# Second layer's row maxima: one of each two key blocks as a difference, its positive part on ScalarE, sum and maximum in one VectorE instruction

## The chip, the cores and the metric

The kernel runs on one core of one Trainium2 chip, in one launch. The metric is device time in microseconds (us): the median of several runs. A profiled execution gives the span from the first to the last instruction, and times below that are given as places ("at 1178.66 us") are us from the start of that span.

## The reference

Two transformer layers on 2048 tokens of 128 channels, all in fp32. The first is causal softmax attention with 16 heads of 8 channels and a linear layer; the second, where the change lies, is linear attention and then an attention whose heads mix experts. Cut to what matters here (8 heads, 5 experts, head size 64):

```python
q5 = (x @ Wq).reshape(b, t, H, E, DH)                 # k5 and v5 likewise from Wkv
q = jnp.einsum('bthed,bthe->bhtd', q5, sd_g)          # experts summed under gates
k = jnp.einsum('bthed,bthe->bhtd', k5, ss_g)
v = jnp.einsum('bthed,bthe->bhtd', v5, ss_g)
attn = jax.nn.softmax(jnp.einsum('bhid,bhjd->bhij', q * scale, k), axis=-1)
out = jnp.einsum('bhij,bhjd->bihd', attn, v)          # then Wo under a mask, summed over experts
```

The softmax is over 2048 keys of each query, without a causal mask, and subtracts each query's maximum before the exponential.

## The kernel before

Each engine runs its own list of instructions in order, and semaphores tie them. The order is set by one list of steps, `SEQ1` for the second layer: every engine walks through it and issues its part of each step. The list is merged from a regular foreground and from preparation steps that carry places in time (`preparation1`, `merge`). Those places come from numbers written by hand (`PROJ1`, `STAGE1`, `MAX1`).

The unit of the foreground is one S step: for a chunk of 512 queries, two tiles of 128 keys. TensorE makes two 128x512 blocks of scores, each from a main product (L775) and a correction product that also adds minus the row maximum (L776). ScalarE takes the exponential of both in one instruction of 1024 columns (L960). Two units later the V step multiplies with the values (L786), and in the D step VectorE adds 704 of the 1024 columns to the running denominator (L1283) and GpSimd the other 320 (L1383). A chunk has 8 units and a head 4 chunks, so 32 units a head and 256 in all. After a chunk, the F step transposes and divides the result, and GpSimd multiplies it with the mask and adds it to `z` (L1394, L1398).

Beside head h's units the kernel prepares head h+1: 48 "proj" steps (three 320-column products each, L747 to L749, and a VectorE product with the gates, L1238), expert sums on GpSimd (L1367 to L1370), a rounding and a difference (ScalarE L933, L935 as step "hi", VectorE L1250, L1251 as "lo"), transposes (step "t", L581, evacuated by ScalarE, L944, L945), and once per head VectorE splits the next weights in two parts (step "w", L1230, L1231).

The maxima are preparation steps too. For each of the 16 query tiles of a head, and each of the 4 blocks of 512 keys, TensorE makes one 128x512 block of approximate scores (L759) and VectorE reduces it to one column of `mxp1` (L1256): 64 such "max" steps a head. Step "m" takes the maximum over a tile's columns (L1268, L1269), and step "q2" transposes it into `q2T`.

The results of all steps but S and V share a ring of three PSUM banks (4, 5 and 7). TensorE may start a ring step only when the step three places earlier in the ring has been read out of its bank:

```python
def take(ring, step):
    turn = ring.turn[step]
    if turn >= len(RING):
        wait_read(pe, ring, ring.order[turn - len(RING)])
    return ring.bank(step)
```

Before the change VectorE reads "proj", "max", "F" and "y" steps, ScalarE "t", "q2" and "zt" steps.

## Time and profile before

| | |
|---|---|
| median of 3 runs | 1859.26 us (1854.18 to 1868.14) |
| span of the profiled execution | 1857.2 us |
| the second layer's exponentials, first to last start (trace) | 798.7 to 1823.7 us |
| TensorE matmul busy | 1645.3 us (89%) |
| VectorE busy | 1435.4 us (77%) |
| ScalarE busy | 782.5 us (42%) |
| GpSimd busy | 878.0 us (47%) |

The profile gives no time for what lies around the span of the profiled execution; the median of the runs is 2.1 us above that span. In the trace heads repeat: from the first exponential of one head to that of the next it is 133.1 or 133.2 us for heads 1 to 5. A share of busy time is an average over stages, so the stretch of one head is what to read: what TensorE waits for in it, and how long.

Engines in the rows: PE is TensorE (PEld its weight loads), DVE is VectorE, ACT ScalarE, POOL GpSimd. In a row of the timeline `[3.92 <-DVE mxp L1256]` says that the engine sat idle for 3.92 us before it, until that instruction released it.

### The profile page before, as it was taken

The numbers are of one execution on the slowest core, as the hardware profiler recorded it, in microseconds if no ns is written. First come the engines' busy times: TensorE is split into PE (matmuls) and PEld (weight loads), VectorE is DVE, ScalarE is ACT, GpSimd is POOL, SyncE is SP. The second block draws the span as 40 slices with busy tenths as digits, with TensorE's granted clock in tenths as the row PEclk, the third lists the DMA queues.
The fourth block names the chain that finished last, engine by engine and source line by source line (L and its number), as shares of the span: only waits on it lengthen the run. The fifth ranks groups of instructions, "written<-read, shape, count | busy, mean of one in ns | idle before, by whom it ended". The sixth has DMA issues, their size and how long they took to land.

```text
span 1857.2 us, 26270 instructions
## 1 busy us (share of the span) xinstructions
PE 1645.3 (89%) x8612; PEld 999.3 (54%) x8612; DVE 1435.4 (77%) x2387; ACT 782.5 (42%) x1046; POOL 878.0 (47%) x906
## 2 busy tenths in 40 slices
PE   3899999999999672699899899899999899899997
PEld 2555555555554361566466466466565565565554
DVE  4996785785786369888888888888898888988862
ACT  3457557567556320223433434334334234234441
POOL 2710000000000024358678589589588587687654
PEclk9799999999999775889899999999999999999996
DMA  2000000000000000000000000000000000000000
GB/s 58 1 1 1 1 1 1 1 1 1 1 1 1 11 1 11 0 11 1 11 1 2 11 1 1 11 1 1 12 1 1 11 1 1 1 1 1 1 11 13
DMA packets 12224, 9.34 MB, mean 5 GB/s; under 512 B 3840, under 2 KB 11584, under 8 KB 12096
## 3 DMA queue, kind: packets, MB, share of 16 engines
q1 hardware_dynamic: 12096, 7.66, 1.5%
q8 instruction: 77, 1.26, 0.3%
q14 instruction: 51, 0.42, 0.1%
HBM read 6.61 MB, written 1.05 MB: 4 GB/s over the span
## 4 chain that ended last, share of the span: by engine, by line
PE 66%; DVE 19%; issue 7%; POOL 5%; ACT 2%; SPq 0%; DMA 0%; DVEq 0%; POOLq 0%; ACTq 0%
PE ps L786 10%; PE ps L606 8%; PE ps L623 7%; PE ps L638 7%; PE ps L759 6%; PE ps L581 5%; PE ps L775 4%; PE ps L776 4%; DVE den L1283 3%; PE ps L747 3%; DVE mxp L1256 3%; PE ps L749 2%; PE ps L748 2%; POOL z L1398 2%; PE ps L797 2%
## 5 line engine op out<-in xcount | busy, mean ns | idle before, releaser
L960 ACT ACTIVATE pbuf<-ps 128x1024 f32<-128x1024 f32 x256 | 262.1, 1024 | 524.0 <-PE ps L776 520.9
L1074 DVE TENSOR_REDUCE mxp<-ps 128x1 f32<-128x512 f32 (+3 forms) x560 | 354.2, 671 | 112.2 <-PE ps L606 56.2
L1256 DVE TENSOR_REDUCE mxp<-ps 128x1 f32<-128x512 f32 x512 | 342.5, 682 | 66.8 <-PE ps L759 66.1
L875 ACT ACTIVATE pbuf<-ps 128x1024 f32<-128x1024 f32 (+3 forms) x320 | 281.7, 896 | 199.1 <-PE ps L626 98.5
L1283 DVE TENSOR_TENSOR den<-den,pbuf 128x704 f32<-128x704 f32 x224 | 292.0, 1303 | 1.1
L786 PE MATMUL ps<-pbuf,h_v 128*64 128x512 f32 x1024 | 284.4, 634 | 0.0
L759 PE MATMUL ps<-k1T,q1T 128*128 128x512 f32 x512 | 223.4, 453 | 38.7 <-DVE mxp L1256 25.1
L1383 POOL TENSOR_TENSOR den<-den,pbuf 128x320 f32<-128x320 f32 x224 | 235.0, 1049 | 42.1 <-ACT pbuf L960 26.5
L606 PE MATMUL ps<-kM,qT 128*128 128x512 f32 (+3 forms) x640 | 243.6, 427 | 9.5 <-ACT kM L862 4.3
L1238 DVE TENSOR_TENSOR gt<-ps,gate 128x320 f32<-128x320 f32 x384 | 182.6, 484 | 54.8 <-PE ps L749 51.7
L623 PE MATMUL ps<-qT,kM 128*128 128x512 f32 (+3 forms) x640 | 207.7, 399 | 8.4 <-ACT pbuf L875 8.4
L775 PE MATMUL ps<-q1T,k1T 128*128 128x512 f32 x512 | 209.4, 409 | 2.3 <-ACT q2T L950 2.3
L776 PE MATMUL ps<-q2T,k2T 65*128 65x512 f32 x512 | 204.6, 400 | 0.0
L606 PEld LDWEIGHTS ps<-kM,qT 128*128 128x128 f32 x640 | 122.4, 197 | 118.7 <-DVE mxp L1074 88.7
L747 PE MATMUL ps<-wh,xh 128*128 128x320 f32 x384 | 136.1, 355 | 53.5 <-DVE gt L1238 36.9
L1367 POOL TENSOR_TENSOR gs<-gt 128x384 f32<-128x384 f32 x120 | 148.3, 1236 | 67.0 <-DVE gt L1238 65.3
L759 PEld LDWEIGHTS ps<-k1T,q1T 128*128 128x128 f32 x512 | 98.8, 194 | 146.3 <-DVE mxp L1256 87.0
L638 PE MATMUL ps<-pbuf,stagev 128*32 128x512 f32 (+3 forms) x1280 | 152.0, 547 | 0.0
L747 PEld LDWEIGHTS ps<-wh,xh 128*128 128x128 f32 x384 | 73.5, 191 | 142.1 <-DVE gt L1238 68.7
L1325 POOL TENSOR_SCALAR rstd<-meanvar 128x4 f32<-128x4 f32 x12 | 2.7, 227 | 304.5 <-DVE meanvar L995 304.5
L1340 POOL COPY stagev<-qkv 128x512 f32<-128x512 f32 x4 | 2.9, 722 | 288.8 <-PE ps L638 266.1
L623 PEld LDWEIGHTS ps<-qT,kM 128*128 128x128 f32 x640 | 117.9, 195 | 35.4 <-ACT pbuf L875 22.9
(212 smaller groups left out, 2484.3 us busy)
## 6 DMA issues: line engine op xcount, KB each, us to landing
wraw<-in_Wkv SPq DMA_DIRECT2D x16, 160.0 KB, 2.6
wraw<-in_Wq SPq DMA_DIRECT2D x8, 160.0 KB, 2.3
out<-x SPq DMA_DIRECT2D x4, 256.0 KB, 2.3
wqkv<-in_wqkvT SPq DMA_DIRECT2D x1, 192.0 KB, 4.0
masks<-in_masks SPq DMA_DIRECT2D x1, 128.0 KB, 4.1
dft<-in_dft SPq DMA_DIRECT2D x1, 128.0 KB, 2.3
wout<-in_Wo SPq DMA_DIRECT2D x2, 64.0 KB, 2.6
ident<-in_ident SPq DMA_DIRECT2D x1, 64.0 KB, 5.7
```

What stands on the lines that cost most here:

```text
L606: mm = pe.matmul(ps[:, bank, w * a:w * (a + 1)], qT[:, g % 2, P * it:P * (it + 1)], kM[g % 2][:, h + a, CH * b:CH * b + w], start=True, st ...
L623: mm = pe.matmul(ps[:, b, off:CH], kM[g % 2][:, h, P * jt:P * (jt + 1)], qT[:, g % 2, CH * c + off:CH * (c + 1)], start=True, stop=jt < TP ...
L638: mm = pe.matmul(ps[32 * h:32 * h + 32, ACC, off:CH], stagev[:, g % 2, jt, h, :], pbuf0[:, u % NP0, h % 2, off:CH], start=jt == 0, stop=jt ...
L747: pe.matmul(o, xh[:, t], wh[:, j, :], start=True, stop=False)
L759: pe.matmul(ps[:, bank, :], q1T[:, h % 2, P * it:P * (it + 1)], k1T[:, h % 2, CH * b:CH * (b + 1)], start=True, stop=True).then_inc(s_turn ...
L775: pe.matmul(ps[:, b, :], k1T[:, h % 2, t], q1T[:, h % 2, q], start=True, stop=False)
L776: mm = pe.matmul(ps[:, b, :], k2T[0:D1 + 1, h % 2, t], q2T[0:D1 + 1, h % 2, q], start=False, stop=True)
L786: mm = pe.matmul(ps[64 * i:64 * i + 64, ACC, :], h_v[:, h % 2, 2 * m + i, :], pbuf1[:, u % NP1, i, :], start=m == 0, stop=m == M1 - 1, til ...
L875: nc.scalar.activation(pbuf0[:, u % NP0, :, off:CH], ps[:, b:b + 2, off:CH], ACT.Exp, scale=float(D0) ** -0.5).then_inc(s_exp, 1)
L1074: v.tensor_reduce(mxp[:, i, h:h + n, b], ps[:, ring0.bank(step), 0:w * n].rearrange("p (h k) -> p h k", h=n), AX.X, ALU.max).then_inc(s_re ...
L1256: v.tensor_reduce(mxp1[:, it % TPC, b:b + 1], ps[:, ring1.bank(step), :], AX.X, ALU.max).then_inc(s_read1d, 1)
L1283: v.tensor_tensor(dn, dn, w, ALU.add).then_inc(s_den1, 1)
```

## The change

For each query tile the four key blocks become two pairs. Of a pair, block a and block b, GpSimd forms the difference of the transposed keys, `kd` = a - b (a new step "kd", twice a head). TensorE multiplies the queries with `kd` (step "dif") and with b (step "max"). ScalarE takes the positive part of the first, which is PSUM to SBUF (`relu`, two slots). VectorE then adds the scores of b and takes the maximum along the row in one instruction: max(a, b) = b + max(a - b, 0). So a head has 32 "dif" and 32 "max" steps, in the ring as 64 steps like before, and half of them are read by ScalarE. In the order a tile's "dif" stands one step ahead of the "max" before it. `mxp1` has two columns a tile instead of four. To make room, some small tensors that are dead by then share their memory with `relu` and `kd`, and `sq2` has 65 columns instead of 128. S, V, D, F, proj and t steps stay as they are.

```diff
@@ preparation1
+            if c % 2:
+                out.append((end + STAGE1[2] + 0.65, ("kd", h, c // 2)))
...
-            items = [("max", h, TPC * c + i, b) for i in range(TPC) for b in range(NC)]
+            pairs = [(h, TPC * c + i, p) for p in range(NC // 2) for i in range(TPC)]
+            items = [("dif", *pairs[0])]
+            for a, b in zip(pairs, pairs[1:] + [None]):
+                items += [("dif", *b)] if b else []
+                items.append(("max", *a))
@@ build
-        ring1 = Ring(SEQ1, ("proj", "max", "F", "y"), ("t", "q2", "zt"))
+        ring1 = Ring(SEQ1, ("proj", "max", "F", "y"), ("t", "dif", "q2", "zt"))
@@ tensor
-                elif kind == "max":
-                    _, h, it, b = step
+                elif kind in ("dif", "max"):
+                    _, h, it, p = step
                     bank = take(ring1, step)
                     wait_read(pe, ring1, ("t", h, NC - 1, 2))
-                    pe.matmul(ps[:, bank, :], q1T[:, h % 2, P * it:P * (it + 1)],
-                              k1T[:, h % 2, CH * b:CH * (b + 1)], start=True, stop=True).then_inc(s_turn1, 1)
+                    if kind == "dif":
+                        pe.wait_ge(s_kd, NC // 2 * h + p + 1)
+                        keys = kd[:, p, :]
+                    else:
+                        keys = k1T[:, h % 2, CH * (2 * p + 1):CH * (2 * p + 2)]
+                    pe.matmul(ps[:, bank, :], q1T[:, h % 2, P * it:P * (it + 1)], keys,
+                              start=True, stop=True).then_inc(s_turn1, 1)
@@ scalar
+                elif kind == "dif":
+                    i = SLOT1[step[1:]]
+                    wait_turn(act, ring1, step)
+                    if i >= NR:
+                        wait_read(act, ring1, ("max", *PAIR1[i - NR]))
+                    nc.scalar.activation(relu[:, i % NR, :], ps[:, ring1.bank(step), :],
+                                         ACT.Relu).then_inc(s_read1a, 1)
@@ vector
                 elif kind == "max":
-                    _, h, it, b = step
+                    _, h, it, p = step
+                    above = relu[:, SLOT1[h, it, p] % NR, :]
                     wait_turn(dve, ring1, step)
-                    v.tensor_reduce(mxp1[:, it % TPC, b:b + 1], ps[:, ring1.bank(step), :],
-                                    AX.X, ALU.max).then_inc(s_read1d, 1)
+                    wait_read(dve, ring1, ("dif", h, it, p))
+                    v.tensor_tensor_reduce(above, ps[:, ring1.bank(step), :], above, 1.0, LOW, ALU.add, ALU.max,
+                                           accum_out=mxp1[:, it % TPC, p:p + 1]).then_inc(s_read1d, 1)
@@ gpsimd
+                elif step[0] == "kd":
+                    _, h, p = step
+                    wait_read(pool, ring1, ("t", h, 2 * p + 1, 0))
+                    if h:
+                        wait_turn(pool, ring1, ("dif", h - 1, NT - 1, p))
+                    a, b = (k1T[:, h % 2, CH * (2 * p + i):CH * (2 * p + i + 1)].bitcast(F32) for i in range(2))
+                    g_.tensor_tensor(kd[:, p, :], a, b, ALU.subtract).then_inc(s_kd, 1)
```

How the lists of instructions read at three places. In them the program's tensors have their names (`ps` is PSUM), and the last part is the shape.

VectorE before, at the split of the next weights (`wh`, `wl`), behind an F step (`rd`, `on`):

```order
L1291 RECIPROCAL rd<-ps 128x4
L1292 TENSOR_TENSOR on<-ps,rd 128x256
L1256 TENSOR_REDUCE mxp<-ps 128x1
L1230 CAST wh<-wraw 128x960
L1231 TENSOR_TENSOR wl<-wraw,wh 128x960
L1256 TENSOR_REDUCE mxp<-ps 128x1 x2
L1283 TENSOR_TENSOR den<-den,pbuf 128x704
L1256 TENSOR_REDUCE mxp<-ps 128x1 x3
L1283 TENSOR_TENSOR den<-den,pbuf 128x704
```

The same place in the changed kernel:

```order
L1324 RECIPROCAL rd<-ps 128x4
L1325 TENSOR_TENSOR on<-ps,rd 128x256
L1289 ISA relu,mxp<-ps,relu 128x512
L1289 ISA mxp 128x1
L1261 CAST wh<-wraw 128x960
L1262 TENSOR_TENSOR wl<-wraw,wh 128x960
L1289 ISA relu,mxp<-ps,relu 128x512
L1289 ISA mxp 128x1
L1316 TENSOR_TENSOR den<-den,pbuf 128x704
L1289 ISA relu,mxp<-ps,relu 128x512
L1289 ISA mxp 128x1
L1316 TENSOR_TENSOR den<-den,pbuf 128x704
```

The split keeps its place; behind it one block is reduced where two were, and each reduction is now two instructions, the second of one column.

TensorE before, at the same place; L759 are the "max" products, L775 and L776 an S step, L786 a V step:

```order
L802 MATMUL ps<-ones,den 128x1 x4
L759 MATMUL ps<-k1T,q1T 128x512
L775 MATMUL ps<-q1T,k1T 128x512
L776 MATMUL ps<-q2T,k2T 128x512
L775 MATMUL ps<-q1T,k1T 128x512
L776 MATMUL ps<-q2T,k2T 128x512
L759 MATMUL ps<-k1T,q1T 128x512 x2
L786 MATMUL ps<-pbuf,h_v 64x512 x2
L759 MATMUL ps<-k1T,q1T 128x512
```

In the changed kernel:

```order
L826 MATMUL ps<-ones,den 128x1 x4
L783 MATMUL ps<-k1T,q1T 128x512
L799 MATMUL ps<-q1T,k1T 128x512
L800 MATMUL ps<-q2T,k2T 128x512
L799 MATMUL ps<-q1T,k1T 128x512
L800 MATMUL ps<-q2T,k2T 128x512
L783 MATMUL ps<-kd,q1T 128x512
L783 MATMUL ps<-k1T,q1T 128x512
L810 MATMUL ps<-pbuf,h_v 64x512 x2
L783 MATMUL ps<-kd,q1T 128x512
```

The products keep their number and places; every other one reads `kd`. In both lists an S step follows, and then two more products of this kind.

GpSimd in the changed kernel, where the first `kd` of a head stands, between the expert sums of two tiles; before, the same rows stood without it:

```order
L1400 TENSOR_TENSOR gs<-gt 128x384
L1401 TENSOR_TENSOR gsum<-gs 128x192
L1402 TENSOR_TENSOR h_qk<-gsum,gt 128x2x64
L1403 TENSOR_TENSOR h_v<-gsum,gt 128x64
L1410 TENSOR_TENSOR kd<-k1T 128x512
L1423 TENSOR_TENSOR den<-den,pbuf 128x320
L1400 TENSOR_TENSOR gs<-gt 128x384
L1401 TENSOR_TENSOR gsum<-gs 128x192
```

The other rows kept their order. In `SEQ1` the last "dif" step of the head before that reads the same part of `kd` is the sixth ring step behind this place, and the instruction waits for it.

## Rows read from the trace of the kernel before

**Rows 1.** Two stretches: length, busy us of PE, PEld, DVE, ACT, POOL; last PEclk, DMA.

```profile
1063.10:1196.20 133.10, 123.27 (x593) 76.64 (x592) 113.81 (x171) 49.41 (x64) 101.53 (x108) 0.99 0.01 5
...
1595.60:1722.70 127.10, 121.31 (x594) 76.04 (x592) 107.92 (x169) 49.45 (x65) 100.76 (x107) 1.00 0.00 1
```

**Rows 2.** Groups by line and shape, 1063 to 1196 us, one head's stretch.

```profile
L1256 DVE TENSOR_REDUCE mxp<-ps 128x1 f32<-128x512 f32 x65 | 43.7, 682 | 7.3 <-PE ps L759 7.3
L1283 DVE TENSOR_TENSOR den<-den,pbuf 128x704 f32<-128x704 f32 x28 | 36.5, 1303 | 0.1
...
L960 ACT ACTIVATE pbuf<-ps 128x1024 f32<-128x1024 f32 x32 | 32.8, 1024 | 67.6 <-PE ps L776 67.4
...
L1388 POOL TENSOR_TENSOR den<-den 128x512 f32<-128x512 f32 x4 | 5.2, 1298 | 10.3 <-DVE den L1283 10.1
...
L945 ACT ACTIVATE q1T<-ps 128x512 fp32r<-128x512 f32 x4 | 2.3, 582 | 0.0
...
L1268 DVE TENSOR_REDUCE mx<-mxp 128x4 f32<-128x16 f32 x4 | 0.7, 163 | 0.1
```

**Rows 3.** TensorE's waits, 1063 to 1196 us: total, times, longest us.

```profile
PE ps L759 <- DVE mxp L1256: 3.9, 1, 3.9
PE ps L747 <- DVE mxp L1256: 1.4, 1, 1.4
PE ps L759 <- DVE gt L1238: 1.3, 1, 1.3
PE ps L581 <- DVE sq L1251: 1.1, 1, 1.1
...
PE ps L581 <- DVE mxp L1256: 0.5, 1, 0.5
```

**Rows 4.** Timeline, 1173 to 1192 us: start, us, engine, what, [idle before].

```profile
1178.66 2.42 DVE L1230 CAST wh<-wraw 128x960 fp32r<-128x960 f32 x1
...
1181.12 3.73 DVE L1231 TENSOR_TENSOR wl<-wraw,wh 128x960 fp32r<-128x960 f32 x1
1181.20 0.39 PE L776 MATMUL ps<-q2T,k2T 65*128 65x512 f32 x1
...
1184.77 1.28 DVE L1256 TENSOR_REDUCE mxp<-ps 128x1 f32<-128x512 f32 x2
...
1185.51 1.18 PE L759 MATMUL ps<-k1T,q1T 128*128 128x512 f32 x2 [3.92 <-DVE mxp L1256]
...
1186.62 1.98 PE L786 MATMUL ps<-pbuf,h_v 128*64 128x512 f32 x4
...
1189.04 0.88 DVE L1283 TENSOR_TENSOR den<-den,pbuf 128x704 f32<-128x704 f32 x1
1189.11 0.63 PE L775 MATMUL ps<-q1T,k1T 128*128 128x512 f32 x1
```

**Rows 5.** Timeline, 1077 to 1091 us.

```profile
1078.93 2.93 POOL L1398 TENSOR_TENSOR z<-z,onm 128x1280 f32<-128x1280 f32 x1
...
1079.41 3.21 DVE L1283 TENSOR_TENSOR den<-den,pbuf 128x704 f32<-128x704 f32 x1
...
1083.28 0.42 PE L747 MATMUL ps<-wh,xh 128*128 128x320 f32 x1 [1.43 <-DVE mxp L1256]
```

**Rows 6.** Timeline, 1133 to 1148 us.

```profile
1134.99 0.86 POOL L1383 TENSOR_TENSOR den<-den,pbuf 128x320 f32<-128x320 f32 x1
...
1136.13 0.39 PE L759 MATMUL ps<-k1T,q1T 128*128 128x512 f32 x1
...
1137.09 1.02 POOL L1367 TENSOR_TENSOR gs<-gt 128x384 f32<-128x384 f32 x1 [1.23 <-DVE gt L1238]
...
1146.26 1.00 POOL L1367 TENSOR_TENSOR gs<-gt 128x384 f32<-128x384 f32 x1 [0.51 <-DVE gt L1238]
```

**Rows 7.** Timeline, 780 to 801 us, before the first head.

```profile
782.92 5.47 DVE L1256 TENSOR_REDUCE mxp<-ps 128x1 f32<-128x512 f32 x9 [4.93 <-PE ps L759]
```

More of the change, by code:

```diff
@@ L46 @@
 NS = 2
+NR = 2
+LOW = -3e38
 M1 = NT // 2
@@ L182, in build @@
         ones = sbuf(ctx, "ones", [P, 1])
-        wgate = sbuf(ctx, "wgate", [P, 2, H1 * E1])
         wout = sbuf(ctx, "wout", [P, 3, D])
-        wlin = sbuf(ctx, "wlin", [P, 4, D])
-        blin = sbuf(ctx, "blin", [P, 3, D])
-        bqcol = sbuf(ctx, "bqcol", [P, 1])
-        stdp = sbuf(ctx, "stdp", [P, 3, H0])
-        blockm = sbuf(ctx, "blockm", [P, D])
-        bd = sbuf(ctx, "bd", [P, 2, D])
-        bsum = sbuf(ctx, "bsum", [P, H0])
-        lden = sbuf(ctx, "lden", [P, 2, TPC, H0])
+        small = ExitStack()
+        sm = lambda name, shape, dt=F32: sbuf(small, name, shape, dt)
+        wgate = sm("wgate", [P, 2, H1 * E1])
+        wlin = sm("wlin", [P, 4, D])
+        blin = sm("blin", [P, 3, D])
+        bqcol = sm("bqcol", [P, 1])
+        stdp = sm("stdp", [P, 3, H0])
+        blockm = sm("blockm", [P, D])
+        bd = sm("bd", [P, 2, D])
+        bsum = sm("bsum", [P, H0])
+        lden = sm("lden", [P, 2, TPC, H0])
+        small.close()
+        relu = sbuf(ctx, "relu", [P, NR, CH])
+        kd = sbuf(ctx, "kd", [P, NC // 2, CH], F32R)
+        sq2 = sbuf(ctx, "sq2", [P, TPC, D1 + 1])
         l0 = ExitStack()
@@ L273, in build @@
         rd1 = s1("rd1", [P, TPC])
-        mxp1 = s1("mxp1", [P, TPC, NC])
+        mxp1 = s1("mxp1", [P, TPC, NC // 2])
         mx1 = s1("mx1", [P, TPC])
@@ L278, in build @@
         sq1 = s1("sq1", [P, TPC, P])
-        sq2 = s1("sq2", [P, TPC, P])
         k1T = s1("k1T", [P, 2, T], F32R)
@@ L340, in build @@
         s_st1 = sem("s_st1")
+        s_kd = sem("s_kd")
         s_m1 = sem("s_m1")
@@ L412, in build @@
         ring0 = Ring(SEQ0, ("max", "F", "pj", "mix", "lin"), ("k", "q", "q2", "at", "lt", "lt2"))
-        ring1 = Ring(SEQ1, ("proj", "max", "F", "y"), ("t", "q2", "zt"))
+        ring1 = Ring(SEQ1, ("proj", "max", "F", "y"), ("t", "dif", "q2", "zt"))
+        PAIR1 = [step[1:] for step in SEQ1 if step[0] == "dif"]
+        assert PAIR1 == [step[1:] for step in SEQ1 if step[0] == "max"]
+        SLOT1 = {pair: i for i, pair in enumerate(PAIR1)}
         def wait_read(eng, ring, step):
```

## The prediction

> **What bounds the kernel now.** I read the second layer by heads, since heads repeat, and asked first which engine has no slack in one head. The windows view gives one head's stretch: 133.1 us, with TensorE busy for 123.3, VectorE for 113.8, GpSimd for 101.5 and ScalarE for 49.4 [rows 1]. So TensorE is nearest to a bound, and it idles for 133.1 - 123.3 = 9.8 us a head. VectorE idles for 19.3 us, yet it is what TensorE waits for. The view of the waits puts a name to TensorE's idle time: 3.9 us in one wait for a block's maximum, 1.4 in another, 1.3 for a product with the gates, 1.1 for the "lo" difference, 0.5 for one more maximum [rows 3]; that is 8.2 of the 9.8. These are five single events a head, not a small delay at each block. A change that halves VectorE's work on the maxima cannot buy its busy time back, only what it takes from these five places.
>
> The largest is the split of the next weights. In the timeline VectorE starts the cast at 1178.66, the subtraction at 1181.12, and its next maximum only at 1184.77. Such lengths come with GpSimd at work beside it, as a sum shows that took 3.21 us from 1079.41 while GpSimd added to `z` from 1078.93 to 1081.86, and 0.88 us elsewhere [rows 4, 5]. TensorE runs on until its three banks are full, stops behind the product of 1181.20 and comes back at 1185.51, after 3.92 us. Behind that it is slow too: the V step of 1186.62 takes 1.98 us, the product of 1189.11 0.63 us where one of the same size took 0.39 at 1181.20 [rows 4]. A head without this split in its stretch takes 127.1 us, with a granted clock of 1.00 instead of 0.99 [rows 1]. So the split costs 133.1 - 127.1 = 6.0 us: 3.9 us of idle time and 2.1 us of what comes behind it (half clock, and VectorE's backlog).
>
> **What the change removes and adds, in busy time.** VectorE loses 64 reductions a head at 0.68 us, 43.7 us in all [rows 2]. It gets 32 fused ones. No row shows that instruction. Its lower bound is the reduction of the same 512 columns, 0.68 us. The built program has a second instruction of one column behind each; the smallest reduction in the trace takes 0.16 us [rows 2]. So one costs 0.68 to 0.84 us, and I take 0.8, since both instructions stand in the list. 32 x 0.8 = 25.6 us: VectorE falls by about 18 us a head. An upper bound, if the fused one worked at half the rate of the reduction, is 2 x 0.68 = 1.36 us: 43.5 us, nothing saved. I take the lower end because the fused one, too, goes once through 512 columns.
>
> The Trainium skill ("VectorE: DVE Perf Modes", section "Two Vector instructions with no wait between them") says that an operation which also writes out its accumulator is two instructions, the main one and an accumulator read. The list shows the same; it gives no time.
>
> ScalarE gets 32 instructions of 512 columns from PSUM, 0.58 us each [rows 2]: 18.6 us, to 68 of 133. That is hidden unless one stands in front of an exponential that TensorE needs; the exponentials wait for TensorE for 67.4 us a head [rows 2], so there is room. The skill ("ScalarE: Activation LUTs", "Rules for kernel authors") advises VectorE and not ScalarE for relu, as up to three times faster in bf16. For this fp32 PSUM source the rows say 0.58 on ScalarE against 0.68 for a VectorE reduction; by that rule the move would be a loss, by the rows it is not.
>
> GpSimd gets two subtractions of 512 columns a head, 1.30 us each like L1388 [rows 2]: 2.6 us, to 104. TensorE's work stays: 64 products, the same sizes and places.
>
> **What of it lies on the path,** event by event, for one head.
> - The split. Behind it, before the change, the first product that must wait is the one whose bank the first "max" behind the cast holds. Now that place in the ring holds a "dif", which ScalarE reads, and the wait moves one product on. So about 0.25 us of the idle time goes (TensorE does one more product, 0.23 to 0.3 us, inside it). Behind the wait VectorE has one block less to catch up with before the denominator and one after it, and V follows one product earlier; of the 2.1 us behind the wait I take 1.2 as gained. Together 1.5 us. Bounds: 0.25, and 6.0 if all of it went.
> - The two waits of 1.4 and 1.3 us come from the denominator sum that GpSimd holds up, like the one of 3.21 us. TensorE then waits for the maximum behind the sum until 1083.28 [rows 5]. In the new order that place is a "max" again, so VectorE still reads it. Nothing is gained, and the longer instruction costs 0.1 us each: +0.2.
> - The wait of 1.1 us for "lo" hangs on GpSimd's sums and ScalarE's "hi"; VectorE comes to it a little earlier, -0.3 (bounds 0 and 1.1).
> - The wait of 0.5 us: the bank is now that of a "dif". It goes, -0.5.
>
> Sum: -1.5 + 0.2 - 0.3 - 0.5 = -2.1 us a head, for the six heads that have a split in their stretch: -12.6. The seventh (127.1 us) has the rest of it: -0.6. The last head has no preparation beside it: 0. Before the first head 16 reductions stand in a row, (5.47 - 0.68) / 8 = 0.60 us from one to the next [rows 7], 9.6 us. As eight pairs they hang on the chain of positive part, product, fused maximum, since the slots of `relu` are two and bank and slot come free late: two pairs to a round of 0.58 (ScalarE), 0.63 (a product at half clock, rows 4) and 0.8 us, with three hand-overs that I estimate at 0.05 to 0.1 us each: 1.1 a pair, 8.8 us: -0.8, of which the split inside them takes some, -0.5. In all 12.6 + 0.6 + 0.5 = 13.7 us: the span 1857.2 becomes 1843.5, and with the 2.1 us by which the median lies above the span 1845.6, rounded to **1845**.
>
> **GpSimd's wait.** The first `kd` of a head is the edit that adds a wait. GpSimd comes to its place at 1134.99, but the last "dif" of the head before that reads the old one is the sixth ring step behind that place; the product that stands there before the change starts at 1136.13 and takes 0.39 us [rows 6], so the wait is 1.5 us, and the work 1.3. Queued behind it stand a denominator sum (the buffer is needed again three units later) and the expert sums, for which VectorE's products wait. So GpSimd is 2.8 us late, and it has 1.23 us of idle time at 1137.09 and 0.51 at 1146.26 [rows 6] to take it in: it remains 1.1 us late. What it feeds next, through `z`, the last sums and "hi", is the "lo" wait above, and there VectorE's own two sums stand in front. I cost it at nothing; without that cover it is 1.1 us a head.
>
> **Rivals.**
> - *GpSimd becomes the bound* (slower). Place: from the first `kd` to the transposes of the last chunk. Price: the whole 2.8 us a head if the idle time of 1.23 and 0.51 is no longer there, since VectorE hands its products over sooner and GpSimd then works without a pause; seven heads make +20, and the gain of the fused maximum is lost in the same wait: 1857 + 20 + 2 = 1879. It decides once GpSimd's slack behind `kd` is under 1.7 us. For it: it is busy for 101.5 us of the 133.1 [rows 1]. Against: none of TensorE's waits is for GpSimd directly [rows 3]. The Trainium skill ("SBUF — State Buffer", "Terms") says that VectorE and GpSimd share one pair of SBUF ports, held exclusively for a whole instruction, the loser blocked. The 3.21 against 0.88 us [rows 4, 5] agree; by it each `kd` can also block a VectorE sum for up to 1.3 us, 16 x 1.3 = 21 us if every one did.
> - *VectorE's relief works further than I count* (faster). The maxima also shorten the lag with which VectorE enters the blocked sums, and if TensorE's idle time behind the split is short enough its clock stays up: the 1.98 us V step would take about half. Then the split gives 3.5 instead of 1.5, the two waits of 2.7 us give half, 1.3: another 3.5 us a head, x 6.5 = 23: 1822.
> - *No change in time:* the fused instruction takes 1.37 us, or the new waits between the three engines eat the 2 us a head: 1859.
>
> **Chances.** Forecast (1838 to 1853) 0.42, relief works further (1815 to 1840) 0.27, no change (1853 to 1868) 0.18, slower (1868 to 1890) 0.13. The range 1820 to 1868 leaves out the slower case and the low end of the second one, some 0.2. A measurement of this kernel tells about 1% from no change, 18.6 us. Faster by over 1% (below 1840.7): the second case and a small part of the first, 0.34. Slower by over 1% (above 1877.9): 0.09. Within: 0.57.
>
> **What would show it.** In the profile after: VectorE's group of maxima at 0.7 to 0.85 us x 256 with a small one beside it; VectorE busy near 96 us and ScalarE near 68 us of a head's stretch; the stretch at about 131 us; the wait behind the split at 3.5 to 3.7 us, those of 1.3 and 1.4 us still there, that of 0.5 us gone; GpSimd's `kd` with a wait of about 1.5 us before it. I am wrong if the fused instruction takes over 1 us, if TensorE shows waits for ScalarE's relu, if the clock stays up behind the split, or if GpSimd's delay reaches TensorE.

## The result, and the profile after

The changed kernel takes 1879.08 us (median of 4 runs, 1869.69 to 1881.08) against 1858.97 us for the kernel before on the same chip (4 runs): ratio 1.0103, 95% interval [1.0063, 1.0144]. It is slower by 1%, outside the predicted range and on the other side of the forecast.

The page of the changed kernel (in all views `...` stands for rows left out): first busy time of the engines, then three groups of its list (count, busy us, mean ns, idle time before).

```profile
PE 1657.1 (88%) x8612; PEld 1010.1 (54%) x8612; DVE 1295.3 (69%) x2387; ACT 921.0 (49%) x1302; POOL 902.0 (48%) x922
...
L1289 DVE CUSTOM_DVE_ANT_0 relu<-ps,relu 128x512 f32<-128x512 f32 x256 | 175.3, 686 | 146.9 <-PE ps L783 144.6
...
L976 ACT ACTIVATE relu<-ps 128x512 f32<-128x512 f32 x256 | 151.5, 595 | 180.5 <-PE ps L783 119.1
L799 PE MATMUL ps<-q1T,k1T 128*128 128x512 f32 x512 | 212.7, 415 | 21.4 <-ACT q2T L981 21.4
```

The work moved as intended: VectorE fell from 1435 to 1295 us. But TensorE waits 21.4 us in front of the main score product for the `q2T` copy (line 981), a wait that cost 0.3 us a head before. One head by the windows view (length; busy us of PE, PEld, DVE, ACT, POOL; granted clock), to be held against [rows 1]:

```profile
1069.40:1206.90 137.50, 125.81 (x594) 78.50 (x592) 96.33 (x171) 66.47 (x96) 104.21 (x110) 0.96 0.02 4
```

The head is 137.5 - 133.1 = 4.4 us longer. TensorE is idle for 11.7 us instead of 9.8 (+1.9), and its own work takes 125.8 instead of 123.3 (+2.5), since the mean granted clock fell from 0.99 to 0.96: more of the work ran at 1.2 GHz, the lower of the clock's two levels. TensorE's waits in that head (total, times, longest), against [rows 3]:

```profile
PE ps L783 <- DVE mxp L1289: 3.7, 1, 3.7
PE ps L799 <- ACT q2T L981: 3.0, 2, 2.8
PE ps L600 <- DVE gt L1269: 1.5, 1, 1.5
PE ps L766 <- DVE mxp L1289: 1.5, 1, 1.5
PE ps L783 <- DVE gt L1269: 1.2, 1, 1.2
```

The split's wait went from 3.9 to 3.7, the waits of 1.4 and 1.3 are still there, those of 1.1 (for "lo") and 0.5 are gone. The one of 1.5 in front of L600, a transposition, was 0.7 before. New is one of 2.8 us for `q2T`. Its cause stands in the timeline, 1141 to 1175 us (start, us, engine, instruction, idle before it):

```profile
1145.30 1.29 POOL L1410 TENSOR_TENSOR kd<-k1T 128x512 fp32r<-128x512 f32 x1 [1.54 <-PE ps L783]
...
1162.06 3.52 POOL L1438 TENSOR_TENSOR z<-z,onm 128x1280 f32<-128x1280 f32 x1
1165.66 1.54 POOL L1400 TENSOR_TENSOR gs<-gt 128x384 f32<-128x384 f32 x1
1167.28 1.31 POOL L1401 TENSOR_TENSOR gsum<-gs 128x192 f32<-128x192 f32 x1
1168.67 0.98 POOL L1402 TENSOR_TENSOR h_qk<-gsum,gt 128x128 f32<-128x128 f32 x1
1169.62 0.31 POOL L1403 TENSOR_TENSOR h_v<-gsum,gt 128x64 f32<-128x64 f32 x1
...
1169.96 0.63 ACT L957 ACTIVATE sk<-h_qk 128x512 fp32r<-128x512 f32 x1 [2.68 <-POOL h_v L1403]
1170.50 0.40 ACT L959 ACTIVATE sq<-h_qk 128x256 fp32r<-128x256 f32 x1
1170.86 1.02 ACT L991 ACTIVATE pbuf<-ps 128x1024 f32<-128x1024 f32 x1
1171.91 0.59 ACT L981 ACTIVATE q2T<-ps 1x512 fp32r<-1x512 f32 x1
...
1172.64 0.72 PE L799 MATMUL ps<-q1T,k1T 128*128 128x512 f32 x1 [2.83 <-ACT q2T L981]
```

Read it backwards. TensorE waits for a copy of 0.59 us. The copy's own input, the transposed shifts, was there at 1168.8; it stands in ScalarE's queue behind an exponential and the "hi" rounding, and "hi" waited 2.68 us for GpSimd's last sum. GpSimd was late: its first `kd` waited 1.54 us and worked 1.29, and then GpSimd had no pause until here. The same place in the kernel before, with no idle time in front of "hi":

```profile
1158.71 0.32 POOL L1370 TENSOR_TENSOR h_v<-gsum,gt 128x64 f32<-128x64 f32 x1
...
1159.05 0.63 ACT L933 ACTIVATE sk<-h_qk 128x512 fp32r<-128x512 f32 x1
...
1161.91 0.47 PE L775 MATMUL ps<-q1T,k1T 128*128 128x512 f32 x1 [0.31 <-ACT q2T L950]
```

The product behind the wait takes 0.72 us instead of 0.47 and the next ones 0.63: the half clock that the split's wait brings stands here a second time.

Not all of the 4.4 us comes from this wait. 20 us into the head TensorE waits 1.5 us for a maximum, as it did before (1.4). Here the clock then falls to half; in the kernel before, and in the changed kernel's own head 3 (heads counted from 0), it stays up. The first two rows are 7 us behind that wait in heads 2 and 3 of the changed kernel, the third is the same place before, and the last is the whole of head 3:

```profile
1089.40:1096.40 7.00, 6.77 (x25) 4.31 (x27) 5.21 (x13) 2.49 (x4) 6.37 (x10) 0.76 0.01 2
1226.90:1233.90 7.00, 6.80 (x32) 4.33 (x33) 6.40 (x16) 3.05 (x5) 6.69 (x10) 1.00 0.00 0
...
1083.10:1090.10 7.00, 6.82 (x33) 4.34 (x34) 6.95 (x14) 1.02 (x1) 6.69 (x11) 1.00 0.00 0
...
1206.90:1342.70 135.80, 125.02 (x593) 77.86 (x592) 95.27 (x171) 66.59 (x96) 104.84 (x110) 0.96 0.02 5
```

By this early half clock head 2 is 2.4 us late at its next common wait (the one of 1.2 us for the gates' product ends 59.6 us into the head instead of 57.2; 0.8 of the 2.4 is the longer wait in front of L600), before GpSimd comes to `kd` at all. Head 3, without it, is 135.8 us: 2.7 us longer than before, 1.0 of idle time and 1.7 of slower clock. Of heads 1 to 6 of the changed kernel four have the early half clock, of the kernel before none.

### The profile page after: what moved, and what is told of

Same layout as the page of the kernel before. It is cut to its first block, busy times and chain, and to the rows that moved or that the text cites. A ratio compares the mean times of both kernels' runs of the same rounds, so it can differ in the third digit from the quotient of the medians.

```text
span 1879.3 us, 27066 instructions
## 1 busy us (share of the span) xinstructions
PE 1657.1 (88%) x8612; PEld 1010.1 (54%) x8612; DVE 1295.3 (69%) x2387; ACT 921.0 (49%) x1302; POOL 902.0 (48%) x922
## 4 chain that ended last, share of the span: by engine, by line
PE 65%; DVE 13%; POOL 10%; issue 7%; ACT 3%; SPq 0%; DMA 0%; DVEq 0%; POOLq 0%; ACTq 0%
PE ps L810 10%; PE ps L625 8%; PE ps L642 7%; PE ps L657 6%; PE ps L783 6%; PE ps L799 4%; PE ps L800 4%; PE ps L600 4%; PE ps L766 3%; POOL z L1438 3%; PE ps L768 2%; PE ps L767 2%; DVE mxp L1105 2%; PE ps L821 2%; POOL onm L1434 2%
## 5 line engine op out<-in xcount | busy, mean ns | idle before, releaser
L991 ACT ACTIVATE pbuf<-ps 128x1024 f32<-128x1024 f32 x256 | 262.2, 1024 | 255.9 <-PE ps L800 254.2
L810 PE MATMUL ps<-pbuf,h_v 128*64 128x512 f32 x1024 | 289.5, 645 | 0.0
L1289 DVE CUSTOM_DVE_ANT_0 relu<-ps,relu 128x512 f32<-128x512 f32 x256 | 175.3, 686 | 146.9 <-PE ps L783 144.6
L1423 POOL TENSOR_TENSOR den<-den,pbuf 128x320 f32<-128x320 f32 x224 | 228.3, 1019 | 40.7 <-ACT pbuf L991 26.5
L976 ACT ACTIVATE relu<-ps 128x512 f32<-128x512 f32 x256 | 151.5, 595 | 180.5 <-PE ps L783 119.1
L799 PE MATMUL ps<-q1T,k1T 128*128 128x512 f32 x512 | 212.7, 415 | 21.4 <-ACT q2T L981 21.4
L783 PE MATMUL ps<-kd,q1T 128*128 128x512 f32 x256 | 111.3, 440 | 26.4 <-DVE mxp L1289 23.4
```

The source lines that it names most:

```text
L799: pe.matmul(ps[:, b, :], k1T[:, h % 2, t], q1T[:, h % 2, q], start=True, stop=False)
L810: mm = pe.matmul(ps[64 * i:64 * i + 64, ACC, :], h_v[:, h % 2, 2 * m + i, :], pbuf1[:, u % NP1, i, :], start=m == 0, stop=m == M1 - 1, til ...
L991: nc.scalar.activation(pbuf1[:, u % NP1, :, :], ps[:, b:b + 2, :], ACT.Exp, scale=float(D1) ** -0.5).then_inc(s_exp1, 1)
L1423: g_.tensor_tensor(dn, dn, w, ALU.add).then_inc(s_den1p, 1)
```

## The experiments

Times are medians; each ratio is to the kernel before on the same chip, with its 95% interval. The experiments ran on several chips, so small differences between two of them are read from the ratios.

**1. Which part of the new steps costs?** First (e1) no `kd` step at all: the "dif" product reads the first key block itself, so the maxima aren't the reference's.

```diff
-            if c % 2:
-                out.append((end + STAGE1[2] + 0.65, ("kd", h, c // 2)))
...
-                        pe.wait_ge(s_kd, NC // 2 * h + p + 1)
-                        keys = kd[:, p, :]
+                        keys = k1T[:, h % 2, CH * 2 * p:CH * (2 * p + 1)]
```

> The changed kernel without the kd steps: TensorE's dif products read the first key block itself instead of the difference, so the maxima are not the reference's; everything else of the change stays (ScalarE's positive part, the fused instruction, the order). Theory A (GpSimd's wait and work for kd make it late, ScalarE's hi waits for its sums, and q2's evacuation is queued behind hi): TensorE's wait of 2.8 us for q2T is gone, the stretch of a head falls from about 137 to 131 to 132 us, time 1840 to 1850. Rival B (the loss is the new chain ScalarE to VectorE and ScalarE's longer queue): 1870 to 1880, TensorE's waits as in the changed kernel.

1857.29 us, 0.9982 [0.9961, 1.0002]. This is above theory A's 1840 to 1850: the `q2T` wait is 1.7 us and not gone. Then (e2) the step stays and only the head's first `kd` moves, by six units:

```diff
-                out.append((end + STAGE1[2] + 0.65, ("kd", h, c // 2)))
+                out.append((u - 10.4 if c == 1 else end + STAGE1[2] + 0.65, ("kd", h, c // 2)))
```

> The changed kernel with the first kd of a head placed 6 units later, behind the last expert sums, where the dif products that it waits for are long issued; same work on GpSimd. Theory A: the wait before kd is gone and its 1.3 us stand behind the sums for which hi waits, so nearly as e1: 1842 to 1855. If GpSimd's or the shared ports' total work counts (rival C, port time), it stays at 1870 to 1880.

1856.39 us, 0.9983 [0.9963, 1.0003]. Both take back the whole loss, and no more. So the 1% is the place of one GpSimd instruction, not its work; rival C, by which GpSimd's or the shared port's total work counts, fell with e2, where the work is the same. TensorE's longest `q2T` wait falls from 2.8 to 1.7 us. In heads without the early half clock the late `kd` saves 2.8 us (133.0 against 135.8; 1.2 of idle time, 1.6 of clock).

Then (e6) one GpSimd instruction later instead of six units:

```diff
-                out.append((end + STAGE1[2] + 0.65, ("kd", h, c // 2)))
+                out.append((end + STAGE1[2] + (1.65 if c == 1 else 0.65), ("kd", h, c // 2)))
```

> The changed kernel with the head's first key difference one GpSimd instruction later, behind the next 0.87 us denominator add instead of in front of it. In the changed kernel this step waited 1.54 us and worked 1.29 us. Theory A (the wait in GpSimd's queue is what is too much, the work fits the slack of 1.23 + 0.51 us that lies behind it): the wait shrinks to about 0.7 us, lateness behind the slack 0.7 + 1.3 - 1.7 = 0.2 us instead of 1.1; TensorE's wait for the q2T copy falls from 2.8 us towards the 1.7 us of the kernel with the step moved away, time 1857 to 1862. Theory B (the 1.3 us of work in that stretch costs wherever it stands): q2T wait stays above 2.4 us, time 1872 or more.

With the step behind the next denominator sum only, its wait fell from 1.54 to 0.7 us: 1857.68 us, 1.0012 [0.9996, 1.0028]. The `q2T` wait is 2.1 us in six heads and 2.4 in one. That is only 0.7 us less than in the changed kernel, but the two heads without the early half clock take 132.6 and 132.8 us instead of 135.8: behind the shorter wait their clock stays up. Moving GpSimd's step by one instruction is worth 17 us (by the ratios) to 21 (by the medians); the time is theory A's, and its reason, that the wait before `kd` is what is too much, fits.

Next (e4), `kd` alone in the kernel before, unused:

```diff
+            if c % 2:
+                out.append((end + STAGE1[2] + 0.65, ("kd", h, c // 2)))
...
+                    if h:
+                        wait_turn(pool, ring1, ("max", h - 1, NT - 1, 1) if p else ("max", h - 1, 13, 3))
...
+                    g_.tensor_tensor(kd[:, 0, :], a, b, ALU.subtract).then_inc(s_kd, 1)
```

> The kernel before with the two kd subtractions alone, at the same places with the same waits, their result used by nobody. Theory A: the same late sums, a wait for q2T appears, heads of 136 to 139 us, 1870 to 1885. Rival B: as the kernel before, 1859.

1905.69 us, 1.0246 [1.0215, 1.0277], outside both theories, and this can't be taken as half of the change: in the old list the wait in front of the first `kd` is 5.6 us, not 1.54. Nor does the `q2T` wait of theory A appear (0.4 us). The lateness comes to TensorE by another engine: VectorE's product with the gates waits for GpSimd's sums, and TensorE for that product.

```profile
1152.32 1.28 POOL L1381 TENSOR_TENSOR kd<-k1T 128x512 fp32r<-128x512 f32 x1 [5.60 <-PE ps L763]
...
1156.96 0.49 DVE L1242 TENSOR_TENSOR gt<-ps,gate 128x320 f32<-128x320 f32 x1 [3.90 <-POOL h_v L1374]
...
1157.51 0.50 PE L763 MATMUL ps<-k1T,q1T 128*128 128x512 f32 x1 [2.07 <-DVE gt L1242]
```

The head is 140.8 us long with the clock at 0.93.

**2. Is it only ScalarE's queue?** The changed kernel with "hi" behind the `q2T` copy (e3):

```diff
-            out += [(end + STAGE1[0], ("hi", h, c)), (end + STAGE1[1], ("lo", h, c))]
+            out += [(u - 8.55 if c == 3 else end + STAGE1[0], ("hi", h, c)), (end + STAGE1[1], ("lo", h, c))]
```

> The changed kernel with the last hi step of a head placed behind q2 instead of before it, in all engines' lists; kd as it is. Theory A in its second half (q2T waits only because it is queued behind hi on ScalarE): TensorE's wait for q2T of 2.8 us is gone, but the transposes behind lo come as late as before, so part of it returns there, at L600: 1860 to 1870. Rival B or C: no change, 1879.

1887.04 us, 1.0153 [1.0128, 1.0177]: slower, outside both theories. "hi" is out of the way, and the wait is the same, in its timeline:

```profile
1168.33 4.87 POOL L1423 TENSOR_TENSOR den<-den,pbuf 128x320 f32<-128x320 f32 x5
1169.30 1.02 ACT L991 ACTIVATE pbuf<-ps 128x1024 f32<-128x1024 f32 x1 [3.57 <-POOL den L1423]
1170.35 0.59 ACT L981 ACTIVATE q2T<-ps 1x512 fp32r<-1x512 f32 x1
...
1171.08 0.77 PE L799 MATMUL ps<-q1T,k1T 128*128 128x512 f32 x1 [2.82 <-ACT q2T L981]
```

My theory of the queue was half right: GpSimd's lateness has two ways to the copy. The exponential in front of it needs a buffer that GpSimd's denominator sum still reads.

**3. Can VectorE take work from GpSimd?** It adds 832 of 1024 denominator columns instead of 704, on top of the late `kd` (e9).

```diff
-SHARE = 704
+SHARE = 832
```

> The changed kernel with the first key difference late (as in e2) and VectorE adding 832 of the 1024 denominator columns instead of 704, GpSimd 192 instead of 320. Theory A (GpSimd is what is late in the second half of a head, and VectorE has the time): GpSimd's add falls from 0.87 to about 0.6 us, nine of them stand in the stretch in question, so its sums come about 2 us earlier, TensorE's 1.7 us wait for the q2T copy shrinks below 0.5 us; 1.5 to 2.5 us a head, time 1838 to 1848. Theory B (the wait is set by ScalarE's or TensorE's own order): q2T wait stays at 1.5 us or more, time 1853 to 1860.

1872.15 us, 1.0092 [1.0079, 1.0104]: slower. The longest `q2T` wait is 1.8 us, as theory B has it, but the time is outside both theories. GpSimd's adds to the denominator fell from 1.07 to 0.86 us each, but the sums beside them grew. Lines view, 930 to 1730 us, of the run with the late `kd`:

```profile
L1316 DVE TENSOR_TENSOR den<-den,pbuf 128x704 f32<-128x704 f32 x168 | 222.6, 1325 | 1.9
...
L1401 POOL TENSOR_TENSOR gsum<-gs 128x192 f32<-128x192 f32 x96 | 67.0, 697 | 7.5
```

and with the larger share:

```profile
L1316 DVE TENSOR_TENSOR den<-den,pbuf 128x832 f32<-128x832 f32 x163 | 222.7, 1366 | 1.8
...
L1401 POOL TENSOR_TENSOR gsum<-gs 128x192 f32<-128x192 f32 x96 | 69.7, 726 | 7.5
```

A theory that fell: columns handed from GpSimd to VectorE don't bring GpSimd's last sums forward. That the two engines hold each other up fits these rows. Most of the loss lies elsewhere: the wait for a maximum 20 us into the head grew from 1.4 to 1.5 or 1.6 us, and the early half clock stands behind it in all six of heads 1 to 6, against three of them with the late `kd` alone. These six heads are 11.0 of the 15.6 us by which the two profiled runs differ.

**4. Why does the rest of the change give nothing?** Without the loss by `kd` the forecast 14 us should show; the ratios of e1 and e2 give 3, with intervals that reach no change. By the profiled runs heads 1 to 6 of e2 are even 9.2 us longer than before (802.0 against 792.8), which the stretches ahead of and behind them make up. Relief alone (e10): the kernel before with reductions over 128 columns.

```diff
-                    v.tensor_reduce(mxp1[:, it % TPC, b:b + 1], ps[:, ring1.bank(step), :],
+                    v.tensor_reduce(mxp1[:, it % TPC, b:b + 1], ps[:, ring1.bank(step), 0:P],
```

> The kernel before with every reduction over 128 of the 512 columns of its product (the maxima of the other columns are left out, so the shifts differ from the reference's). This relieves VectorE by about 0.35 us in each of 64 reductions, some 22 us a head, more than the change did (18 us), with no work added on ScalarE or GpSimd and every instruction in its place. Theory A (VectorE's relief is worth nothing where the waits stand: the weights' split is one block behind work that waits for TensorE, and the wait for the last chunk's low parts turns into one for GpSimd's sums): waits of 9.6 us a head become 8 to 9, time 1848 to 1857, ratio 0.995 to 1.000. Theory B (the relief works as forecast, about 2 us a head and the tail, and only what the change adds eats it): 1830 to 1843, ratio 0.985 to 0.992.

1832.8 us, 0.9868 [0.9845, 0.9891]. Theory A fell: relief of VectorE is worth 24 us by the runs. Of the 24.2 us by which the profiled runs differ, though, only 8.0 lie in heads 1 to 6. 5.2 lie in head 0, 5.2 ahead of the first exponential and 5.9 behind the last head's first one; these last two parts differ by as much between other kernels here (790.9 to 798.7 and 128.3 to 134.5 us). In one of its heads (1316.0 to 1446.2 us, 130.2 us long) TensorE's waits are

```profile
PE ps L759 <- DVE mxp L1256: 3.5, 1, 3.5
PE ps L775 <- ACT q2T L950: 1.6, 1, 1.6
PE ps L759 <- DVE gt L1238: 1.2, 1, 1.2
PE ps L747 <- DVE mxp L1256: 1.0, 1, 1.0
```

Here, too, the 1.1 us wait for "lo" has turned into one for `q2T`: so it isn't the new steps that cost this part of the gain. But two waits for maxima are 0.4 us shorter than [rows 3], which is the time by which one reduction is shorter (0.285 against 0.682 us), and two that stood in front of L581, 0.7 us for `gt` and 0.5 for a maximum, are gone. The changed kernel with the late `kd` has 3.7 and 1.4 us for maxima and 0.7 to 1.5 for `gt` there. Next (e14), the fused instruction over 128 columns on top of the late `kd`:

```diff
-                    above = relu[:, SLOT1[h, it, p] % NR, :]
+                    above = relu[:, SLOT1[h, it, p] % NR, 0:P]
...
-                    v.tensor_tensor_reduce(above, ps[:, ring1.bank(step), :], above, 1.0, LOW, ALU.add, ALU.max,
+                    v.tensor_tensor_reduce(above, ps[:, ring1.bank(step), 0:P], above, 1.0, LOW, ALU.add, ALU.max,
```

> The changed kernel with the first key difference late (as in e2), and VectorE's fused instruction over 128 of the 512 columns (the other columns' maxima are left out); ScalarE's positive part stays over 512. Theory A (what kept e2 from the 24 us of e10 is that VectorE's relief came as fewer instructions and not as shorter ones: TensorE waits for single instructions of VectorE's, and the one it waits for still took 0.69 + 0.08 us): time falls by 10 to 18 us against e2, to 1838 to 1846, ratio 0.990 to 0.995 or below. Theory B (ScalarE's 0.60 us in front of each pair's end is what ate it): within 4 us of e2, ratio 0.996 to 1.000.

1840.62 us, 0.9895 [0.9872, 0.9919], as theory A has it. And the positive part over 128 columns as well (e16):

```diff
-                    nc.scalar.activation(relu[:, i % NR, :], ps[:, ring1.bank(step), :],
+                    cols = CH if i < NR else P
+                    nc.scalar.activation(relu[:, i % NR, 0:cols], ps[:, ring1.bank(step), 0:cols],
```

> e14 with ScalarE's positive part over 128 columns as well (the first two uses of the buffers still over 512). Theory A: no more than 4 us below e14, since ScalarE is idle for half of every unit and its result waits for nothing on VectorE. Theory B: the gain that e14 lacks comes here, 10 us or more below e14, to e10's ratio of 0.987.

1829.83 us, 0.9860 [0.9835, 0.9884]. So 16 us come from the length of VectorE's instruction, and 7 (by the ratios) to 11 (by the medians) more from ScalarE's. The two intervals overlap, so this second part isn't clear of noise: theory A's 4 us is exceeded, theory B's 10 reached by the medians alone. The two runs have the same waits (3.3, 1.5, 1.2, 1.0 us). What differs is the clock, one head of each by the windows view, e14 first:

```profile
1320.20:1453.40 133.20, 125.28 (x593) 77.86 (x592) 85.72 (x170) 66.39 (x97) 107.45 (x110) 0.96 0.02 5
```

```profile
1308.80:1438.90 130.10, 122.28 (x593) 76.90 (x592) 85.37 (x171) 56.36 (x96) 107.56 (x110) 0.99 0.02 5
```

The same TensorE instructions take 125.3 us at a granted clock of 0.96 and 122.3 at 0.99. The late-`kd` kernel shows the same between its own heads:

```profile
1060.60:1197.50 136.90, 126.47 (x593) 78.64 (x592) 96.01 (x171) 66.47 (x96) 105.25 (x110) 0.95 0.02 4
1330.60:1463.60 133.00, 123.45 (x593) 77.18 (x592) 95.44 (x171) 66.45 (x96) 105.40 (x110) 0.97 0.02 5
1080.60:1087.60 7.00, 6.86 (x27) 4.33 (x27) 5.16 (x14) 2.57 (x4) 6.30 (x11) 0.76 0.00 1
1350.60:1357.60 7.00, 6.86 (x33) 4.38 (x34) 6.40 (x16) 3.11 (x5) 6.69 (x10) 1.00 0.00 0
```

Behind the same 1.4 us wait for a maximum, 20 us into the head, the clock goes to half in one head (0.76 over 7 us) and stays up in the other (1.00). Three of heads 1 to 6 are of the longer kind, some 3.5 us each. In e10, e14 and e16, where this wait is 1.0 us instead of 1.4, none of 18 heads is. So most of what e14 gains over e2 lies in these three heads (heads 1 to 6 together: 791.0 against 802.0 us); that the shorter instruction leaves a shorter wait, behind which the clock stays up, fits, but is not shown apart. Why the clock falls behind some waits of 1.4 us and not behind others stays open; the kernel before, with the same wait, has none.

**5. The split.** If it is one block of 6.1 us at a place fixed by the order, it must be moved, not relieved. To unit 24, where VectorE is idle:

```diff
-        out.append((u - U1 - 4, ("w", h)))
+        out.append((u - U1 - 7.4, ("w", h)))
```

> The changed kernel with the first key difference late (as in e2) and the split of the next head's weights moved from unit 28 to unit 24 of a head, where VectorE in e2 is idle for 5 us in a row. Theory A (the time freed on VectorE lies where nothing waits for it, and the 6.1 us split is one block at a place fixed by the order, so that the relief alone can't shorten TensorE's 3.7 us wait there): with the split in the idle stretch the 3.7 us wait and most of the half-clock stretch behind it (2 us) go; a new wait for maxima or a late denominator may cost 1 us; 4 to 5 us in each of 6 to 7 heads, time 1822 to 1835. Theory B (some other resource, such as GpSimd's queue or the clock, sets the period of about 133 us for a head in every kernel so far): time stays at 1850 to 1858.

> The kernel before with the split moved in the same way and nothing else. There VectorE is idle 4.8 us in the four units behind that place against 9.8 us in e2. Theory A (relief of VectorE is worth something once the split stands in idle time): TensorE's 3.9 us wait goes but 1 to 3 us of new waits for maxima come, since maxima and denominators stand behind the split with less slack; time 1830 to 1850, 5 to 15 us above e7. Theory B (the place alone matters, VectorE's load not at all): within 3 us of e7.

> The changed kernel, key differences at their places, with only the weights' split moved from unit 28 to unit 24 as in e7 and e8. Theory A (the early key difference costs by itself, through GpSimd's queue, whatever the split does): 20 us above e7, 1828 to 1838, above e8 (the kernel before with the same move, 1821.6). Theory B (the two costs share a cause, such as the state of the clock behind one long wait): within 8 us of e7, 1813 to 1821.

| kernel, with the split at unit 24 | us | ratio |
|---|---|---|
| late `kd` (e7) | 1812.68 | 0.9775 [0.9761, 0.9789] |
| before (e8) | 1821.60 | 0.9821 [0.9805, 0.9838] |
| changed (e11) | 1827.18 | 0.9831 [0.9810, 0.9853] |

The 3.7 and 3.9 us waits are gone in all three, and the clock stands at 0.99 to 1.00. The early half clock is gone too but for one head of e8. All three came out below their theory A's range; e8 is 8.9 us above e7, as its theory A has it; e11, above e7 by 14.5 us (by the ratios 10, since it ran on another chip), stands between its theories. Inside a head at a clock of 1.00, VectorE's relief gives next to nothing as long as the `q2T` wait of 1.7 us stands there. First e7, then e8:

```profile
918.00:1044.90 126.90, 120.91 (x593) 76.19 (x592) 95.09 (x171) 66.67 (x97) 107.47 (x111) 1.00 0.02 5
...
1046.90:1173.90 127.00, 121.19 (x593) 76.06 (x592) 110.68 (x171) 49.42 (x64) 102.10 (x109) 1.00 0.02 5
```

VectorE is busy for 95.1 against 110.7 us, and the heads differ by 0.1 us. The early `kd` costs 0.6% here, against 1.2% without the move (changed against late `kd`): its price hangs on what else disturbs the head, which fits the clock's part in it.

**6. The copy in front of the exponential.** The last chunk's "q2" half a unit earlier, in both kernels with the early split:

```diff
-            out += [(end, ("m", h, c)), (end + 1, ("q2", h, c))]
+            out += [(end, ("m", h, c)), (end + (0.55 if c == 3 else 1), ("q2", h, c))]
```

> The kernel before with the weights' split at unit 24 and with the last chunk's q2 transposes and ScalarE's copy of them half a unit earlier, in front of the exponential that they stood behind. TensorE's wait for the q2T copy is only 0.3 us there and its wait for the low parts 1.1 us stays: within 5 us of e8, 1815 to 1823.

> e7 (first key difference late, split at unit 24) with the last chunk's q2 step half a unit earlier, so that ScalarE copies the shifts ahead of the exponential, which waits for GpSimd's denominator. Theory A (the 1.7 us wait for that copy is all that GpSimd's lateness costs there, and it stands behind the exponential only by order): the wait falls to 0.3 us or less, no wait for low parts comes back since VectorE is early; 1.4 to 2.5 us in each of seven heads, time 1795 to 1804, and 12 us or more below e12. Theory B (TensorE is held by GpSimd at the next step anyway: the transposes that need the same sums): the wait only moves to the transposes, time 1808 to 1815.

Before with both moves (e12): 1816.07 us, 0.9773 [0.9750, 0.9795], as expected. Late `kd` with both (e13): **1800.3 us, 0.9687 [0.9665, 0.9709]**, 3.1% faster than before, theory A's time and the best here. Its waits in a head of 125.4 us:

```profile
PE ps L766 <- DVE mxp L1289: 1.4, 1, 1.4
PE ps L783 <- DVE gt L1269: 1.2, 1, 1.2
PE ps L600 <- DVE gt L1269: 0.7, 1, 0.7
...
PE ps L799 <- ACT q2T L981: 0.2, 1, 0.2
```

and those of the kernel before with the same moves, 127.0 us:

```profile
...
PE ps L581 <- DVE sq L1269: 1.0, 1, 1.0
PE ps L581 <- DVE gt L1238: 0.7, 1, 0.7
PE ps L581 <- DVE sq L1251: 0.6, 1, 0.6
PE ps L581 <- DVE mxp L1256: 0.5, 1, 0.5
```

Only now does the relief pay inside a head: the three waits of 1.0, 0.6 and 0.5 us for VectorE are absent from the first list, the head is 1.6 us shorter at the same clock of 1.00, and the two kernels are 15.8 us apart.

## Why the prediction was wrong

The forecast was 1845 us (its sum of 1845.6 rounds to 1846, which changes nothing), and 1879 was measured. By the ratios about 22 us of the difference are `kd` at its place (1.0103 against 0.9983), and about 11 are relief that did not come.

- **The step that failed** is "I cost it at nothing; without that cover it is 1.1 us a head". The wait of 1.5 us and the work of 1.3 came as forecast (1.54 and 1.29), and so did the idle times that take them in. But I named the "lo" sums as the place where the lateness arrives and VectorE's own sums as cover. It arrives one step earlier, at ScalarE: "hi" waits there for GpSimd's last sum, the exponential for a buffer that GpSimd's denominator sum still reads, and the `q2T` copy queued behind both is one that TensorE needs. I followed GpSimd's consumers but not what stands in line behind the consumer. e2 (same work, another place: 22 us less by the ratios) shows that the place is what costs; the way to the copy is read from the timeline, and e3 shows that "hi" alone is not the whole of it.
- **The size** was too small too. By the rows 2.8 us minus 1.23 and 0.51 of slack leaves 1.1; `z` took 3.52 instead of 2.91 us and the sum behind it 1.31 instead of 0.59, which would make 2.4. From the place of `kd` to the end of its last sum GpSimd took 26.2 us instead of 24.0, so 2.2. And a wait of TensorE's isn't paid at its length: of the 2.8 us that the place of `kd` costs in heads without the early half clock, 1.6 are slower clock.
- **The rival "GpSimd becomes the bound"** named the place and gave 1879, with a chance of 0.13. That the number agrees is luck in part: it has the whole 2.8 us of GpSimd's delay as time of TensorE's, and of the 2.8 measured only 1.2 are idle time. The slack of 1.74 us was used up, but the forecast had that too; that VectorE's earlier products took it away, the rival's condition, no run shows. Against the rival I had set that none of TensorE's waits is for GpSimd directly. That is no evidence. A wait is put down to the last engine of a chain.
- **"The split", 1.5 us of 2.1 a head,** gave 0.2 (3.9 to 3.7). VectorE had been waiting for TensorE in front of it (idle 1.03 us, released by line 802, in the kernel before), so it wasn't late, and its 6.1 us stayed. The wait did move one product on, as forecast. e7, e8 and e11 show that the place is worth 1.8 to 2.7%. In the forecast this wait was the largest row of the profile, and I asked what the change does to it, not what it would take to remove it.
- **"lo" and the 0.5 us wait:** both went, 1.6 us, more than the 0.8 that I counted; in their place came the `q2T` wait, 1.7 us even with the late `kd`.
- **The clock at 20 us into a head** is in no term of the forecast. The changed kernel falls to half behind the wait of 1.4 or 1.5 us there in four of heads 1 to 6, with the late `kd` in three, the kernel before in none. That takes part of e2's relief; the `q2T` wait in place of the "lo" wait takes another, since even a head without the early half clock has 133.0 us against 133.1. So the rival "no change in time" describes e2: its new waits between the engines are there, the clock it does not name.
- **"The two waits of 1.4 and 1.3":** right; 1.5 and 1.2. e10 and e14 fit the reason: TensorE waits for one instruction of VectorE's, and the change made these fewer, not shorter. The wait of 1.4 us became 1.0 only where the instruction was shortened.
- **ScalarE at "hidden":** no wait of TensorE's for the positive part shows. e16 against e14 gives 7 to 11 us for 128 instead of 512 columns, by the clock and not by a wait, with intervals that overlap; whether it costs anything is open.
- **Right:** the fused pair (0.686 + 0.08 = 0.77 us; I took 0.8), VectorE's 96 us and ScalarE's 66 in a head. The start before the first head can't be judged: the first exponential is at 797.2 instead of 798.7 us (-0.5 was forecast), but at 794.1 in e2.

With the order mended around it (e12 to e13) the changed maxima give 15.8 us, near the 13.7 forecast. That is luck: they come from other waits than the forecast's, and 1.5 us of its 2.1 a head was the split.

## What to carry to other kernels

When a step is added to an in-order queue, find what it delays, then list what is queued behind each engine that waits for that, down to the engine that sets the time; here GpSimd's queue and ScalarE's lay between one subtraction and TensorE. Fewer instructions on an engine gave next to nothing here where TensorE waited for the end of a single one, or for a block that starts only after it: shortening that one helped, and so did moving the block into idle time, which was worth about twice what the change cost. Compare heads whose clock ran alike before a difference is put down to a wait. Try an added step at several places before judging a change: one place further on made 17 to 21 us of difference.

## What the runs showed of the hardware

- VectorE's fused add-and-maximum over 512 columns from PSUM and SBUF takes 0.686 us, as long as the plain reduction of one source (0.68), and its accumulator read 0.08 us. At 128 columns it is 0.286 (e14), the reduction 0.285 (e10).
- ScalarE's positive part, 512 fp32 columns from PSUM to SBUF: 0.595 us.
- The granted clock is part of a wait's price. The 593 TensorE instructions of a head took 121.1 us at 1.00, 122.3 at 0.99, 125.3 at 0.96 and 129.9 at 0.93 (e13, e16, e14, e4; e4 is the order of the kernel before, with products of the same sizes).
- Behind the wait 20 us into a head the clock fell to half in none of 18 heads where the wait was 1.0 us (e10, e14, e16), in four of six in the changed kernel (1.4 to 1.5 us), in none of six in the kernel before (1.4 us), and in all six of e9 (1.5 to 1.6 us). So the length of the wait alone does not decide it.
